# SyncE's first loads: a wait for the first weight block, and the third block ahead of the second input

## What is computed

```python
def layer(h, params):
    wl, b_l, ws, b_s, wr, b_r, g, beta = params
    u = jnp.einsum('bid,bjd->bij', h, h) / temper
    a = jax.nn.softmax(u, axis=-1)
    delta = a * adjacency_matrix
    attn = delta / (jnp.sum(delta, axis=-1, keepdims=True) + 1e-10)
    hl = h @ wl.T + b_l
    hs = h @ ws.T + b_s
    hr = h @ wr.T + b_r
    ctx = einsum(attn * upper, hl) + diag_a[..., None] * hs + einsum(attn * lower, hr)
    ...
    return relu(layernorm(ctx) * g + beta)
x = _layernorm(x + two_layers(x, adj), axis=-1)
```

## Time and profile before

| | us |
|---|---|
| median of three runs | 1594.62 |
| lowest and highest | 1594.57, 1594.89 |
| the profiled execution | 1594.88 |
| its span | 1592.9 |
| PE busy in it | 1574.9 (99%) |
| DVE, POOL, ACT busy | 1387.4, 1290.2, 1082.6 |

### The profile page before, as it was taken

How to read it: one execution, slowest core, us unless ns; L and a number is a source line. 1 busy time by engine, 2 the same in 40 slices (tenths; PEclk the granted TensorE clock), 3 DMA queues, 4 the chain that set the end, 5 groups by cost and what they waited for, 6 DMA issues and landing times.

```text
span 1592.9 us, 36013 instructions
## 1 busy us (share of the span) xinstructions
PE 1574.9 (99%) x9273; PEld 1567.8 (98%) x9273; DVE 1387.4 (87%) x4491; ACT 1082.6 (68%) x2958; POOL 1290.2 (81%) x1664
## 2 busy tenths in 40 slices
PE   9999999999999999999999999999999999999996
PEld 8999999999999999999999999999999999999995
DVE  7888888888888888888888888888888888888887
ACT  6676666766676667676667666666667666767665
POOL 5788888888888888888888888888888888888874
PEclk9999999999999999999999999999999999999998
DMA  5555555555555555555555555555555555555541
GB/s 182 129 136 135 136 131 139 130 137 131 138 133 134 131 142 128 135 133 138 128 137 136 134 135 131 136 132 137 132 138 133 134 131 141 129 135 132 135 110 48
DMA packets 589175, 211.28 MB, mean 133 GB/s; under 512 B 473952, under 2 KB 572256, under 8 KB 589152
## 3 DMA queue, kind: packets, MB, share of 16 engines
q1 hardware_dynamic: 490752, 198.91, 48.1%
q10 hardware_dynamic: 98400, 12.11, 4.9%
HBM read 128.98 MB, written 81.92 MB: 132 GB/s over the span
## 4 chain that ended last, share of the span: by engine, by line
PE 96%; DVE 1%; POOL 1%; issue 0%; ACT 0%; DVEq 0%; POOLq 0%; ACTq 0%
PE p_proj L461 74%; PE p_gather L589 16%; PE p_score L455 6%; POOL proj_split L298 0%; POOL w L1354 0%; POOL hT_layer L1333 0%; DVE p_gather L725 0%; DVE p_gather L733 0%; DVE stats L702 0%; DVE p_gather L698 0%; DVE w L836 0%; DVE y L739 0%; POOL rstd L1307 0%; ACT spread L1123 0%; PE p_rows L565 0%
## 5 line engine op out<-in xcount | busy, mean ns | idle before, releaser
L461 PE MATMUL p_proj<-w,hT_layer 128*128 128x384 f32 x6912 | 1339.6, 337 | 0.8 <-DVE w L836 0.8
L461 PEld LDWEIGHTS p_proj<-w,hT_layer 128*128 128x128 f32 x6912 | 1173.8, 188 | 2.0 <-DVE w L836 1.6
L298 POOL TENSOR_TENSOR proj_split<-proj,proj_split 128x768 fp32r<-128x768 f32 x253 | 468.0, 1850 | 10.0 <-ACT proj_split L1064 10.0
L767 DVE TENSOR_TENSOR proj<-p_proj,bias_all 128x768 f32<-128x768 f32 x256 | 243.9, 953 | 94.0 <-PE p_proj L461 93.8
L1307 POOL TENSOR_TENSOR rstd<-veps,neg_half 128x1 f32<-128x1 f32 x384 | 210.7, 549 | 134.2 <-DVE veps L711 54.3
L589 PE MATMUL p_gather<-proj_split,attnT_split 128*128 128x384 f32 x1536 | 308.8, 335 | 1.5 <-issue 1.5
L1303 POOL TENSOR_TENSOR attnT_split<-attnT,attnT_split 128x256 fp32r<-128x256 f32 x256 | 189.7, 741 | 124.9 <-ACT attnT_split L1055 124.8
L589 PEld LDWEIGHTS p_gather<-proj_split,attnT_split 128*128 128x128 f32 x1536 | 270.4, 188 | 2.0 <-issue 2.0
L1064 ACT ACTIVATE proj_split<-proj 128x768 fp32r<-128x768 f32 x256 | 215.2, 841 | 83.5 <-DVE proj L767 82.5
L455 PE MATMUL p_score<-hT_layer 128*128 128x256 f32 x768 | 216.1, 282 | 1.2 <-DVE hT_layer L754 0.8
L1135 ACT ACTIVATE hT_layer<-xt_raw 128x384 fp32r<-128x384 f32 x128 | 67.1, 525 | 189.1 <-issue 187.9
(11 more groups left out here) (71 smaller groups left out, 1669.0 us busy)
## 6 DMA issues: line engine op xcount, KB each, us to landing
swap_mem<-blocks SPq DMA_DIRECT2D x124, 256.0 KB, 2.1
whole<-swap_mem SPq DMA_DIRECT2D x496, 64.0 KB, 2.5
xt_raw<-xT SPq DMA_DIRECT2D x128, 192.0 KB, 2.6
xn<-x SPq DMA_DIRECT2D x128, 192.0 KB, 2.6
out<-o SPq DMA_DIRECT2D x128, 192.0 KB, 2.0
rows_mem<-rows_blocks SPq DMA_DIRECT2D x123, 192.0 KB, 1.9
adj_layer<-adj SPq DMA_DIRECT2D x256, 64.0 KB, 2.1
rowsT<-rows_mem ACTq DMA_DIRECT2D x246, 48.0 KB, 2.5
```

Source lines behind the costliest of these rows:

```text
L298: op.tensor_tensor(proj_split[u][:, LO], proj[u][:, UP:LOW + 1, :], proj_split[u][:, HI].bitcast(F32), ALU.subtract).then_inc(s_proj_lo[k], 1)
L461: return nc.tensor.matmul(p_proj[:, which, 0:D], hT_of(k, b)[:, slot, st, c, :], w[:, k, which, mv, c, :], start=(n == 0), stop=(n == 8))
L767: nc.vector.tensor_tensor(proj[u][:, UP:LOW + 1, :], p_proj[:, UP:LOW + 1, 0:D], bias_all[:, k, UP:LOW + 1, :], ALU.add).then_inc(s_biased ...
```

## The change

SyncE waits for UP to land (its semaphore at 16) after it has issued LOW, and SELF is then issued ahead of input 1 instead of behind it.

```diff
             sp.dma_start(w_raw[:, 0, LOW], WT[0, :, LOW]).then_inc(s_w[0][LOW], 16)
+            sp.wait_ge(s_w[0][UP], 16)
+            sp.dma_start(w_raw[:, 0, SELF], WT[0, :, SELF]).then_inc(s_w[0][SELF], 16)
             sp.dma_start(xt_raw[:, 1], xT[1]).then_inc(s_xt[1], 16)
-            sp.dma_start(w_raw[:, 0, SELF], WT[0, :, SELF]).then_inc(s_w[0][SELF], 16)
             sp.dma_start(bias_all[:, 0, UP:LOW + 1],
                          bias[0, UP:LOW + 1].partition_broadcast(P)).then_inc(s_bias_sides[0], 16)
```

## The result

The changed kernel takes 1596.24 us in the median of 22 runs (1594.15 to 1598.33), the kernel before beside it 1594.01 us in 22 (1593.18 to 1595.75). The ratio over all runs is 1.0012, with a 95% interval of 1.0007 to 1.0018: slower by 0.12%, some 1.9 us, within the 0.2% that the prediction counts as the same. The two medians lie 2.2 us apart. The single execution profiled took 1597.45 us, 1.2 us above the median; what it shows is one of two outcomes that the kernel has, and the spread itself is part of the answer. Of all the runs in this document one, of the kernel with the wait alone, took 1932.87 us at a mean granted clock of 0.752; it is left out of its ratio, and nothing here explains it.

A forecast was written before the change was run, and what follows sets the result against it. The prediction took PE, busy without a gap from 44 to 1500 us, as the bound. Input 1 landing late gave +0.2 us, all else 0: 1594.62 + 0.2 = 1594.8 us, range 1593.5 to 1596.4 us.

The forecast's parts named there:

- the forecast's own 0 to +0.6 us: Band around the predicted +0.2 us for PE's start on SELF; chance 0.48.
- the rival given 0.13: Input 1, issued at 6.2, keeps its old 5.9 us to landing and lands at 12.1: 1597.0 us; chance 0.13.
- What bounds the kernel: PE is busy without a gap from 44 to 1500 us, so a shift at 12 us reaches the end unchanged.
- The wait bites for 2.8 us: SyncE reaches the wait at about 2.65, UP lands at 5.5; SELF issued at about 5.5, input 1 at 6.2.
- Does the line run dry: Whether queued transfers run out before SELF's bytes move at 6.5 us: average gap 0.15 us at most, none taken.
- the sum: Input 1 lands at 9.9 to 9.95 instead of wanted 9.74; PE starts SELF at 12.0: +0.2 us.
- Relief: LOW lands early with loads behind it held back: -0.1 to -1.3 us, best 1593.8 us; chance 0.28.
- the worst case: Input 1 takes the bias load's 7.3 us and lands at 13.5: +3.8 us, 1598.4 us; chance 0.03.

The follow-up runs named there:

- the wait for LOW: Changed kernel with SyncE waiting for LOW instead of UP before issuing SELF; 1599.22 us against 1594.86 for the kernel before, ratio 1.0030.
- the wait for input 0: Changed kernel with SyncE waiting for input 0 instead of UP before issuing SELF; 1594.96 us against 1594.86 for the kernel before, ratio 1.0001.
- the late wait: Kernel before, old order, with SyncE's wait for UP added after SELF's issue, ahead of the biases; 1594.72 us against 1594.77, ratio 0.9999.
- ScalarE's other order: Changed kernel with ScalarE also taking SELF ahead of input 1; 1596.77 us against 1594.46 for the kernel before, ratio 1.0009.

## Why the prediction was right, and where it was not

The time lies in the range, near its upper end. The medians lie 2.2 us apart, the ratio says 1.9 us, where +0.2 was said. That is outside the forecast's own 0 to +0.6 us and in the band of the rival given 0.13; the range held because it took in the nearer half of that rival. There is luck in it: ten of the 22 single runs lie above the range, and the median is within it by how the two outcomes happened to mix.

*What bounds the kernel.* Right. From 44 to 1500 us PE is busy 1455.99 of 1456.00 us after the change, and a shift of PE at the start is still there at the end, give or take the 0.4 us above. Of all profiled executions only the first of the wait alone has more idle time there, 0.57 us.

*The wait bites for 2.8 us.* Right: SELF is issued at 5.41, input 1 at 5.78, 0.37 us later and not 0.7.

*Does the line run dry.* This step failed. The prediction found an average gap of at most 0.15 us and took none for the end of each load. The rows after show 219 GB/s between 6 and 8 us where 392 stood, and the exchange and the wait apart show that only the wait brings it that low. The sum of bytes by an average rate hid two things, which the wait for LOW shows. The end of a load lags behind the bytes: from 6 us on the throughput was down to 46 GB/s in the first microsecond, and LOW was not landed before 7.0. And the rate behind a gap comes back slowly, with 175 GB/s in the second microsecond after SELF's issue. What follows the gap is not a fixed cost but a load that takes 4.0 or 5.5 us. When it takes 4.0, the sum comes out right: input 1 at 9.68 to 9.91 (said: 9.9 to 9.95), PE on SELF at 11.76 to 11.98 (said: 12.0), and 1594.4 to 1594.8 us. In part that is because UP landed, and SELF was issued, at 5.1 to 5.3 there and not at 5.5. When it takes 5.5, the input comes at 11.5.

*A time to landing that goes with the issue.* The rival given 0.13 came true in size in part of the executions: 5.7 us against the 5.9 assumed, PE 1.74 us late against 2.4. Its mechanism did not: the wait for input 0 moved SELF's issue by 0.7 us and its landing by 0.2, and with the wait for LOW input 1 landed 4.3 us after its issue.

*Relief.* The prediction took none, since holding back the loads behind LOW would give it nothing. That was wrong: LOW landed at 7.0 with nothing behind it, and at 7.5 to 7.7 instead of 8.1 in the kernels with the wait for UP. Part of that comes with the exchange, for it landed at 7.8 and 7.7 also where SELF was queued right behind it (the exchange alone, the wait for input 0). It was worth nothing in time, since PE then waits for SELF, a later load, and only waits longer.

*The clock.* The prediction does not name it, and this is its second miss. It priced lateness of PE one to one. Here PE, idle for 2.76 us, lost another 1.3 us to a clock that was halved for 3.4 us.

*The chances.* 0.94 for no change beyond 0.2% fits a loss of 0.12%. The size of the worst case, +3.8 us, did occur in single runs of the changed kernel, which reach 1598.33 and 1599.10 us, 4.3 and 4.2 us above the median beside them. No such run was profiled; that load and clock made it up together, and not the load alone as I had it, is what the profiled ones suggest.

What stays open is why SELF takes 4.0 us in one execution and 5.5 in another, once the transfers have run low; that LOW lands a little earlier in the second kind is all that the rows add. In the old order the two executions had 4.7 and 5.5. No kernel here beats the one before; the exchange, the wait alone, the late wait and the wait for input 0 all tie with it.

## What to carry to other kernels

In these runs a wait ahead of issuing a load cost nothing where what was already queued outlasted the wait and the start of the next transfer; an average over the queue did not tell whether it would, so leave it a margin. Two edits that are each free can cost together when the one uses up the spare time that covers the other: here the exchange took the second input's 1.1 us of slack, and the wait made the landing late. Where TensorE stands for some microseconds at the start, price the clock behind the gap too, and profile several executions, because a median of a kernel with two outcomes describes neither.

## What the runs showed of the hardware that I had not expected

A 576 KB load issued while the transfers ran low took 4.0 to 4.1 us in three executions of one order and 5.1 to 5.6 in four. The load of the second weight block, issued at 2.19 each time, landed at 7.0 where nothing was issued before it had landed, at 7.5 to 7.7 where the next load was issued at 5.1 to 5.6, and at 8.1 where input 1 and then SELF followed at once. TensorE's clock fell to half for 3.4 us after 2.76 us without work, and did not fall where PE waited 1.41 us at one place; it did fall where two waits of 0.79 and 1.28 us had a single product between them (ScalarE's other order). A low part of 128x384 took VectorE 1.04 us beside a GpSimd operation and 0.5 us by itself, so a load 0.5 us late was made good by the operations that no longer met.
